# Edges of a graph network sorted by one-hot products beside the dense layers, instead of by scattering single records

## The reference

```python
edge_index = jnp.stack([src, dst])
x = _layernorm(x + _L0_gnn_ref(x, ..., edge_index), axis=-1)   # two GCN convolutions over all edges and self loops
x = _layernorm(x + _L1_gnn_ref(x, edge_index, ...), axis=-1)   # segment_sum(x[src], dst), then a two-layer MLP
x = _layernorm(x + _L2_gnn_ref(edge_index, edge_type_100, x, ...), axis=-1)
x = _layernorm(x + _L3_gnn_ref(x, ..., src, dst), axis=-1)
...
# in L2, twice, for each half of the edges on its own:
row, col = (idx[0], idx[1])                     # src, dst
m = ccorr(x[col], rel_full[etype]) @ W          # circular correlation by FFT
m = m * norm[:, None]
return jax.ops.segment_sum(m, row, num_segments=n)
```

## Time and profile before

| what | us |
|---|---|
| median of 3 runs (lowest, highest) | 3339.09 (3335.11, 3347.93) |
| the profiled execution: its time, its span | 3336.1, 3334.3 |
| front: start of counting | 213.2 |
| counting | 213.2 to 634.4 |
| sums and preparations | to 697.4 |
| dense layer 1: first product to last post | 697.43 to 762.7 |
| dense layer 2 | 774.96 to 851.7 |
| dense layer 3 | 873.19 to 953.8 |
| tables, but for the records | 957.9 to 977.1 |
| first gather of the first edge layer | 1130.55 |

### The profile page before, as it was taken

One profiled execution on the slowest core, in us unless ns is written; L12 is line 12 of the kernel. 1 busy time (PEld: TensorE's weight loads), 2 busy tenths in 40 slices (PEclk: granted clock), 3 DMA queues, 4 the chain that ended last, 5 costly groups with the idle time before them and its releaser, 6 DMA issues.

```text
span 3334.3 us, 42302 instructions
## 1 busy us (share of the span) xinstructions
PE 1953.3 (59%) x12094; PEld 1522.2 (46%) x12095; DVE 1535.8 (46%) x3964; ACT 1303.1 (39%) x3196; POOL 2292.9 (69%) x2359
## 2 busy tenths in 40 slices
PE   0038888768550286555655555656666666666657
PEld 0036654434230165555655555535555555544544
DVE  7969999623320232222222222345544454444453
ACT  3069876202110074333533343244333353343322
POOL 0777777777777677777777777377777777777700
PEclk9985555578765565555555555578777786787678
DMA  1000000079010132222222222153333333323271
GB/s 38 1 1 2 2 2 2 9 116 130 4 21 1 30 78 55 52 54 52 54 53 53 53 52 49 36 139 82 78 79 78 79 78 80 78 78 76 63 170 42
DMA packets 182963, 183.42 MB, mean 55 GB/s; under 512 B 78966, under 2 KB 155746, under 8 KB 181987
## 3 DMA queue, kind: packets, MB, share of 16 engines
q1 hardware_dynamic: 100657, 99.37, 14.8%
q0 software_dynamic: 75424, 78.83, 10.2%
q10 hardware_dynamic: 6656, 2.40, 0.3%
HBM read 153.48 MB, written 26.94 MB: 54 GB/s over the span
## 4 chain that ended last, share of the span: by engine, by line
POOL 62%; issue 22%; PE 7%; DVE 5%; DMA 3%; PEld 0%; ACT 0%; SPq 0%; PEldq 0%; ACTq 0%; DVEq 0%; POOLq 0%
POOL adj_again_middle L1474 38%; POOL sorted_edges L280 23%; DMA adj_again_middle<-gather_table,gidx_s 2%; PE psum L1594 2%; PE psum L1630 1%; DVE adj_again_middle L1546 1%; PE psum L1098 1%; DMA l_v<-in_L_gnn_beta 1%; PE psum L1095 1%; DVE picked L387 1%; PE psum L2059 0%; DVE runs L422 0%; PEld psum L1630 0%; PE psum L2360 0%; PE psum L1968 0%
## 5 line engine op out<-in xcount | busy, mean ns | idle before, releaser
L1474 POOL DMA_INDIRECT adj_again_middle<-gather_table,gidx_s x1568 | 1508.4, 962 | 540.7 <-issue 471.5
L280 POOL DMA_INDIRECT sorted_edges<-rec,row_i x784 | 782.6, 998 | 335.4 <-issue 255.8
L1594 PE MATMUL psum<-rel_parts,oh_t 128*128 128x96 bf16 (+1 forms) x4704 | 559.0, 286 | 717.0 <-DVE adj_again_middle L1546 562.6
L1546 DVE TENSOR_TENSOR adj_again_middle<-adj_again_middle,psum 128x256 f32<-128x256 f32 x1176 | 442.1, 417 | 1146.1 <-DMA adj_again_middle<-gather_table,gidx_s 852.8
L1514 ACT ACTIVATE adj_again_middle<-cst,lo_s 128x125 f32<-128x125 f32 x1664 | 527.1, 388 | 1074.2 <-PE psum L1630 1070.4
L1594 PEld LDWEIGHTS psum<-rel_parts,oh_t 128*128 128x128 bf16 x4704 | 410.9, 126 | 837.1 <-issue 586.7
L1630 PE MATMUL psum<-adj_again_middle,oh_s 128*125 x3328 | 735.8, 380 | 23.8 <-issue 18.5
L1630 PEld LDWEIGHTS psum<-adj_again_middle,oh_s 128*125 128x125 f32 x3328 | 657.7, 286 | 50.4 <-issue 44.6
L712 PE MATMUL psum<-oh_dst,oh_src 128*125 128x300 bf16 (+2 forms) x784 | 341.5, 527 | 70.7 <-DVE oh_dst L666 44.3
L1518 ACT ACTIVATE oh_s<-adj_again_middle,cst 128x500 f32<-128x500 f32 x416 | 296.1, 712 | 13.6
L712 PEld LDWEIGHTS psum<-oh_dst,oh_src 128*125 128x125 bf16 x784 | 155.8, 199 | 181.4 <-issue 82.9
(11 more groups left out here) (380 smaller groups left out, 1126.8 us busy)
## 6 DMA issues: line engine op xcount, KB each, us to landing
tb<-sorted_types SPq DMA_DIRECT2D x392, 128.0 KB, 3.2
adj_again_middle<-gather_table,gidx_s POOLq DMA_INDIRECT x1568, 2.6
adj_saved<-adj SPq DMA_DIRECT2D x6, 2734.4 KB
sorted_edges<-rec,row_i POOLq DMA_INDIRECT x784
adj_again_middle<-adj_saved SPq DMA_DIRECT2D x3, 2734.4 KB
adj_again_last<-adj_saved SPq DMA_DIRECT2D x2, 2734.4 KB
adj_again_first<-adj_saved SPq DMA_DIRECT2D x1, 2734.4 KB
adj_saved<-adj SPq DMA_DIRECT2D x6, 317.4 KB
```

The lines of the kernel that those rows point to most:

```text
L280: nc.gpsimd.indirect_dma_start(rec_d[c // HC], bass.IndirectOffsetOnAxis(ap=row_i[:, c:c + 1], axis=0), rec[:, c, :], None).then_inc(sent. ...
L1474: nc.gpsimd.indirect_dma_start(gx[g % DEEP][:, k, :], None, table_d[d], bass.IndirectOffsetOnAxis(ap=gidx_s[:, t:t + 1], axis=0),).then_in ...
L1546: mul = v.tensor_tensor(part_prod[:, u * SUB:(u + 1) * SUB, s, :].rearrange("p g (a f) -> p g a f", a=2), rows[:, :, s * d // 2:(s + 1) * ...
L1594: mm = nc.tensor.matmul(ps_rel[:, k * RS:k * RS + W], oh_t[g % (AHEAD + 1)][:, (u * SUB + k) * P:(u * SUB + k + 1) * P], rel_parts[:, s, : ...
```

## The change

Nothing is scattered edge by edge any more. The sorted list gets runs of eight (`RUN`): each block of nodes starts at a multiple of eight, for every two partitions. A chunk of 784 edges (98 partitions of 8, two source partitions) is put in order by products with one-hot matrices: for an edge the target is one of 120 rows (`block_t`) and one of 8 places in it (`place_t`). A record is now five fields of a byte each (two for `src`, two for `dst`, one for the type), stored as int16 after the products. The result, 120 rows of 8 records of 5 fields (80 bytes a row), goes out in one indirect DMA, and there are 128 of them (`SORT_STEPS`), 64 for each half, with two rings: `ONES_RING` 2 for the one-hots, `SENT_RING` 6 for the rows.

- Front: one rank part for each half; the 13 operations for `row_i`, `rec` and both `send_records` go. `bases` has 14 operations (was 5). The five fields are cast (ACT, 3 copies), turned to 98 partitions (PE, 12 turns of 4 transposes) and copied out (ACT, 12 copies of 98x512), then four DVE operations make `block_t` and `place_t`.
- Sums stage: 108 chained DVE operations on 128x120 make the target rows of the runs, two transposes turn them.
- Dense layers: a `steps=` argument; seven steps for each of the chunk slots, 49 in layer 1, 49 in layer 2 and 30 in layer 3. `PROJECTED`, the number of PSUM banks for projections, goes from 4 to 2 there.
- Tables: POOL waits for each half's landings before it reads the records, which are now turned; the types need no transposes, the destinations eight, and those of `make_spans` go. `DST_RING` goes from 8 to 7.

```diff
-                        link(v.tensor_copy(row_i[:, at], rank[:, at]))
...
-                        link(v.tensor_tensor(row_i[:, at], tmp[:, at], mask[:, at], ALU.add))
...
+                    dve.wait_ge(turned_out.sem, 2 * FIELDS + 2)
+                    link(v.tensor_scalar(part_i, slot_i[:], 3, None, ALU.arith_shift_right))
+                    link(v.tensor_copy(block_t[:].rearrange("p s t -> p (s t)"), part_i))
+                    link(v.tensor_scalar(part_i, slot_i[:], RUN - 1, None, ALU.bitwise_and))
+                    link(v.tensor_copy(place_t[:].rearrange("p s t -> p (s t)"), part_i))
...
-        send_records(FIRST_SENT, COLS)
...
+                    for h in range(2):
+                        link(v.tensor_tensor(shifts[:, h, 0:BLOCKS + 1], shifts[:, h, 1:], shifts[:, h, 0:BLOCKS + 1], ALU.subtract))
+                        link(v.tensor_scalar(rows_f[:, h, :], iota[:, 0:MOST_BLOCKS], float(RUN), None, ALU.mult))
+                        for b in range(BLOCKS + 1):
+                            link(v.tensor_scalar(past_f[:], iota[:, 0:MOST_BLOCKS], thresholds[:, h, b:b + 1], shifts[:, h, b:b + 1],
+                                                 ALU.is_ge, ALU.mult))
+                            link(v.tensor_tensor(rows_f[:, h, :], rows_f[:, h, :], past_f[:], ALU.add))
...
+            PROJECTED = 4 if steps is None else 2
+            behind = 2 if hidden else 1
...
+                            if s % 3 == 2 and sorting:
+                                sort_products(pe, sorting.pop(0))
...
+                            for step in steps[c] if steps is not None else ():
+                                sort_out(act, step)
...
+                    for step in [k for c in range(behind) for k in steps[c]] if steps is not None else ():
+                        sort_ones(dve, step)
...
+                        for step in steps[c + behind] if steps is not None and c + behind < CHUNKS else ():
+                            sort_ones(dve, step)
...
+        def sort_ones(dve, step):
+
+            v, u, at = nc.vector, step % ONES_RING, column_of(step)
+            if step >= ONES_RING:
+                dve.wait_ge(sort_done.sem, step - ONES_RING + 1)
+            v.tensor_tensor(place_ones[u][:], iota_b[:, 0:RUN].rearrange("p (a k) -> p a k", a=1).to_broadcast([CH, RUN, RUN]),
+                            place_t[:, at, :].rearrange("p (t a) -> p t a", a=1).to_broadcast([CH, RUN, RUN]),
+                            ALU.is_equal).then_inc(places_made.sem, 1)
+            v.tensor_tensor(block_ones[u][:], iota_b[:].rearrange("p (a k) -> p a k", a=1).to_broadcast([CH, RUN, MOST_BLOCKS]),
+                            block_t[:, at, :].rearrange("p (t a) -> p t a", a=1).to_broadcast([CH, RUN, MOST_BLOCKS]), ALU.is_equal)
+            dve.wait_ge(places_made.sem, step + 1)
+            v.tensor_tensor(placed[u][:], place_ones[u][:].rearrange("p t (k a) -> p t k a", a=1).to_broadcast([CH, RUN, RUN, FIELDS]),
+                            fields_t[:, at, :, :].rearrange("p t (a f) -> p t a f", a=1).to_broadcast([CH, RUN, RUN, FIELDS]),
+                            ALU.mult).then_inc(ones_made.sem, 1)
+
+        def sort_products(pe, step):
+
+            u, to = step % ONES_RING, (6 + step % 2) * BANK
+            pe.wait_ge(ones_made.sem, step + 1)
+            if step >= 2:
+                pe.wait_ge(sort_kept.sem, step - 1)
+            for t in range(RUN):
+                mm = nc.tensor.matmul(psum[0:MOST_BLOCKS, to:to + RUN * FIELDS], block_ones[u][:, t, :],
+                                      placed[u][:, t, :, :].rearrange("p k f -> p (k f)"), start=(t == 0), stop=(t == RUN - 1))
+            mm.then_inc(sort_done.sem, 1)
+
+        def sort_out(act, step):
+
+            act.wait_ge(sort_done.sem, step + 1)
+            if step >= SENT_RING:
+                gone = step - SENT_RING
+                act.wait_ge(landed[gone % 2].sem, 16 * (gone // 2 + 1))
+            to = (6 + step % 2) * BANK
+            nc.scalar.copy(block_rows[step % SENT_RING][:], psum[0:MOST_BLOCKS, to:to + RUN * FIELDS]).then_inc(sort_kept.sem, 1)
...
+            for step in range(SORT_STEPS):
+                h, i = step % 2, step // 2
+                pool.wait_ge(sort_kept.sem, step + 1)
+                if i >= 1:
+                    pool.wait_ge(landed[h].sem, 16 * i)
...
+                nc.gpsimd.indirect_dma_start(
+                    rec_d[h], bass.IndirectOffsetOnAxis(ap=run_rows[:, at:at + 1], axis=0),
+                    block_rows[step % SENT_RING][:], None).then_inc(landed[h].sem, 16)
```

More of the change, by code:

```diff
@@ L12 @@
 U16 = mybir.dt.uint16
+U8 = mybir.dt.uint8
 ALU = mybir.AluOpType
@@ L66 @@
 RUNS = 3
-RANK_PARTS = ((0, 0, HC // 2), (0, HC // 2, HC), (1, 0, HC))
-RANKED_AT = [h * HC + first for h, first, _ in RANK_PARTS]
 CHUNK = 4 * LO
@@ L261, in gnn_stack @@
         records = ExitStack()
[L262 to L264 removed]
+        fields_t = sb("fields_t", [CH, SORT_STEPS, RUN, FIELDS], U8, records)
+        block_t = sb("block_t", [CH, SORT_STEPS, RUN], U8, records)
+        place_t = sb("place_t", [CH, SORT_STEPS, RUN], U8, records)
+        thresholds = sb("thresholds", [P, 2, BLOCKS + 1], F32, records)
+        shifts = sb("shifts", [P, 2, BLOCKS + 2], F32, records)
+        run_rows = sb("run_rows", [MOST_BLOCKS, SORT_STEPS], I32, records)
+        landed = [signal(f"landed{h}") for h in range(2)]
         nat_blk = sb("nat_blk", [P, QUAD * NQ], BF16, records)
@@ L1009, in _ @@
                     mm.then_inc(nodes_turned.sem, 1)
+                    pe.wait_ge(rows_made.sem, 1)
+                    for h in range(2):
+                        mm = nc.tensor.transpose(psum[0:MOST_BLOCKS, 7 * BANK + h * P:7 * BANK + (h + 1) * P], rows_f[:, h, :], ident)
+                    mm.then_inc(rows_turned.sem, 1)
                 @block.scalar
@@ L1096, in third @@
                                                     skip_group_check=True)
+                        sorting = list(steps[c]) if steps is not None else []
                         for s in range(BLOCKS):
@@ new lines, in gnn_stack, with steps_of @@
+        block_rows = [sb(f"block_rows{u}", [MOST_BLOCKS, RUN * FIELDS], I16, dense_room) for u in range(SENT_RING)]
+        places_made, ones_made, sort_done, sort_kept = (
+            signal(n) for n in ("places_made", "sort_ones_made", "sort_done", "sort_kept"))
+        SLOTS_OF_STEPS = 3 * CHUNKS - 2
+        per_slot = -(-SORT_STEPS // SLOTS_OF_STEPS)
+        def steps_of(layer):
+            return [range(min(k * per_slot, SORT_STEPS), min((k + 1) * per_slot, SORT_STEPS))
+                    for k in range(layer * CHUNKS, (layer + 1) * CHUNKS)]
@@ L1430, in gnn_stack @@
             split(parts12, parts3, rem, x[:])
-            dense(counted_adj, parts12, parts3, ident_b, left, room, True, True, [w_sum[:], w_own[:], b1[:], w2[:]], hidden_post)
+            dense(counted_adj, parts12, parts3, ident_b, left, room, True, True, [w_sum[:], w_own[:], b1[:], w2[:]], hidden_post,
+                  steps=steps_of(2))
             normal_end(c, var, mean)
@@ L1900, in comp_layer @@
         def comp_layer(c, n, d, m, feat, fwd, rel_in, y_t, norm, rel_next, make_feat, middle_f32, also=[], loaded=None,
-                       beside=None, after=None):
+                       beside=None, after=None, src_t=None):
             half, W, T = d // 2, 3 * d // 2, 2 * d // P
```

271 lines of the change are left out of this document (145 added, 126 removed).

## The result

The changed kernel takes 3402.27 us (median of 4 runs, 3396.37 to 3414.43) against 3339.38 us: ratio 1.0195 with a 95% interval of 1.0177 to 1.0214, so 63 us slower. The forecast was 3376 us, slower by 37.

What follows compares the result with a forecast made beforehand. POOL's queue was taken to set the end nearly throughout, so the start of the gathers counts. Terms -41 - 9 + 18 + 212 - 148 + 5 = +37 on 3336.1 gave 3373, median 3376 us; own range 3335 to 3415, ends 3290 and 3460.

Steps and rivals of the forecast that it cites:

- the start of counting: Front: less DVE work and an iota no longer behind 96 sends start counting about 41 us earlier.
- counting: Counting stage: without sends L666 isn't disturbed, -9 us, between 0 and -20.
- the wait of 148.2: Before the layer-1 gathers: DVE's wait for the sends goes, -148.2 us.
- Sums stage: Sums stage: 108 chained DVE operations take 38 us, partly in DVE's wait for PE, so it ends 18 us later.
- The turns in the dense stage: Dense layers: program order makes DVE and PE wait for each other, +68, +91 and +30 us, together +189.
- a step: Dense layers: three DVE operations for each of 128 steps, 1.8 us a step after overlap.
- the clock: Dense layers: PE idles in each chunk and restarts slowly, five starts of 3 us, +15.
- Landings: Dense layers: a transfer waits for its half's previous one, +8 us, between 0 and +32.
- Rival 2: Dense layers: landings beside the saving take 8 to 9 us, +24 on the forecast, 3400 us; chance 0.14.
- Rival 1: Dense layers: the 960-element comparison runs at half the slope, a step is 1.3 us, -55, 3321 us; chance 0.24.
- Rival 3: Dense layers: PE's clock stays at 1.2 GHz, some 8 us for each of 18 chunks, +145, 3520 us; chance 0.08.
- Rival 4: Dense layers: sends hold up DVE, 0.19 to 0.96 us a step, +24 to +123, say 3435 us; chance 0.06.

Runs made afterwards that it cites:

- e4: The kernel before without its last 688 sends, waiting only for the first 96: 3737.56 us, slowed by gathers of never filled lists.
- e6: The changed kernel with DVE's steps one chunk further ahead, ACT's layer 2 post before its copy, and the 108 sums operations on POOL: 3325.22 us, ratio 0.9968.
- e2: The changed kernel with the saving of the adjacency moved from beside layers 1 and 2 to beside layer 3: 3408.79 us, ratio 1.0215.
- e12: e9 with the steps dealt out anew, 21, 56 and 51 to the three layers: 3307.95 us, ratio 0.9903.
- e3: The changed kernel without the sort steps, their sends and the waits for landings, so all gathers read row 0: 4023.57 us.
- e8: e6 with the steps dealt out as 14, 49 and 65 to the three layers: 3315.81 us, ratio 0.9937.
- e9: e8 with DVE waiting before each step for its own last operation: 3322.79 us, ratio 0.9948.

## Why the prediction was right

- **What the change takes away.** Right in each term: the start of counting (-44.4 for -41), counting (-10.1 for -9; e4 confirms its cause, the sends, and its place, L666), the wait of 148.2. What the page chain said of POOL held: with POOL out of the way every microsecond of the other engines ahead of the gathers counts.
- **Sums stage.** +16.8 for +18, and e6 takes it back (56.4 us again).
- **The turns in the dense stage.** The mechanism was right. In e2, with no saving beside them, layers 1 and 2 take 142.9 and 191.6 us: +65 and +93 against the kernel before, for +68 and +91. The agreement is partly luck, since two errors cancel: a step was 1.61 us, not 1.8 (98 x 0.19 = 19 us in these two layers), and as much was lost elsewhere. About 10 us of that are PE's lower clock in the stretches in which DVE waits, as e2 shows; where the rest went isn't shown. Layer 3 took 38.7 for 30 and its share of the clock.
- **Landings, the term that was mis-sized.** I took +8 between 0 and +32; e2 measured 30 in layer 1 and 20 in layer 2, 51 in all. The step of the forecast that failed is this one: it gave the landings beside the saving a price near the quiet one, 2.11 us. The landings were 8.4 to 12.1 us, in the chain of waits; with two halves taking turns, and a half's next transfer waiting for its last to land, a step costs about 6 us instead of 3 as long as the saving lasts (six sends of one half start 10.4 to 12.9 us apart). The upper bound was too low as well: it had landings of 8 to 9 us.
- **Rivals.** Rival 2 (landings), to which I gave 0.14, is what came, on top of the turns of the forecast, and its 3400 us is nearer to the 3402 measured than my 3376. Its price of +24 on mine was too low too; the terms that came in under hid that. Rival 1 (a cheap comparison) fell: 1.15 us, on the line; the Trainium skill's rule ("VectorE: DVE Perf Modes", What auto-detection actually checks) agrees. Rival 3 (PE at 1.2 GHz throughout) came in part: a granted 0.69, 0.66 and 0.86 in the three layers. The 10 us above are a part of its price; the whole wasn't tried on its own. Rival 4 (sends hold up DVE) fell: `block_ones` took 1.146 to 1.154 us in all 128 steps. In these rows it is POOL that waits.
- The 25 us that the first gather was later than forecast are thus 43 from the landings (51 less 8), less some 17.5 that the other terms came in under: 3.4 in the front, 1.1 in counting, 1.2 in the sums, 6.6 in the rest of the dense stage and 5.2 behind it.

## What to carry to other kernels

Work that is moved from the queue that bounds the kernel into other stages isn't free there, even where their engines have idle time: look at who must wait for whom in program order. Here the same steps cost 254 us in one order and, with one chunk more of distance and dealt out by what each stage has room for, about 175 (first gather of e12 less that of e3, 159, and the 16 that e12 saves in the sums stage); with the chain of small operations on an idle engine this turned 2% slower into 1% faster. A small transfer that must land before the next is sent should be priced beside the large one that runs at that time, not by its quiet landing.

## What the runs showed of the hardware

- A POOL send beside an unbroken stream of DVE operations with two inputs ends only when the stream does: 13.75 us for 0.99 (e8), and a DVE wait for its own last operation, once in a step, suffices to let sends through in 1.10 us (e9). The Trainium skill ("SBUF — State Buffer", SBUF: two separate sides) tells of a lock for a whole instruction, between such a DVE operation and a GpSimd one that reads SBUF. These rows agree that POOL waits, and go further: 23 operations began and ended under the one send of 13.75 us.
- DVE can be the one to wait elsewhere: its comparisons with one input (L666, 500 columns) took 384 ns on average beside the sends and 349 ns without them (e4).
- Indirect gathers that all read one row are slow. Landing in the changed kernel, median us, and in e3, where the list stays at its zero fill and each node number is 0 (line of the page's part 6; in e4, with 96 of 784 columns filled, it is 27.5):

```profile
adj_again_middle<-gather_table,gidx_s POOLq DMA_INDIRECT x1568, 2.5
```

```profile
adj_again_middle<-gather_table,gidx_s POOLq DMA_INDIRECT x1568, 33.7
```
